# One triangle of X X^T and the zeros of unused rows, in a four-layer image kernel

## The reference, cut to what matters

```python
x = x + L0(_gn(x))   # 1x1 conv to 576, depthwise 3x3/5x5/7x7, 1x1 conv, channel attention with top-k, 1x1 conv
x = x + L1(_gn(x))   # below
x = x + L2(_gn(x))   # selective scan
x = x + L3(_gn(x))   # depthwise 7x7, mirrored borders

def L1(x, w_qkv):    # x: (2, 192, 64, 64), 8 heads of 24 channels
    qkv = jnp.einsum('bchw,oc->bohw', x, w_qkv)
    q, k, v = jnp.split(qkv, 3, axis=1)
    q = _l2norm(q); k = _l2norm(k)                    # over the pixels
    attn = softmax(jnp.einsum('bhcn,bhdn->bhcd', q, k) / sqrt(hw))
    return jnp.einsum('bhcd,bhdn->bhcn', attn, v)
```

## Time and profile before

| | us |
|---|---|
| median of 3 runs | 2481.89 (2481.35 to 2492.42) |
| profiled execution | 2484.08 |
| its span | 2482.2 |
| TensorE busy | 1941.6 (78%) |
| VectorE busy | 1276.3 (51%) |
| ScalarE busy | 804.2 (32%) |
| GpSimd busy | 856.1 (34%) |

### The profile page before, as it was taken

One profiled execution on the slowest core, in us unless ns is written; L12 is line 12 of the kernel. 1 busy time (PEld: TensorE's weight loads), 2 busy tenths in 40 slices (PEclk: granted clock), 3 DMA queues, 4 the chain that ended last, 5 costly groups with the idle time before them and its releaser, 6 DMA issues. The chain is left out here.

```text
span 2482.2 us, 36929 instructions
## 1 busy us (share of the span) xinstructions
PE 1941.6 (78%) x15660; PEld 1208.7 (49%) x15660; DVE 1276.3 (51%) x1317; ACT 804.2 (32%) x1269; POOL 856.1 (34%) x452
## 2 busy tenths in 40 slices
PE   3789899769999999999977867777677767775042
PEld 1477776667777777777734422222222222221032
DVE  5445454441111111111172055799999999998613
ACT  2345455440000000000042125733543444334610
POOL 3234333430000000000000040499899989994000
PEclk9889899889999999999988878899889988998565
DMA  8899999969242323221030031588778868873799
GB/s 292 264 347 318 345 326 345 357 214 242 63 117 62 105 75 93 87 82 39 1 102 11 0 116 44 133 204 213 183 198 221 214 163 220 210 187 108 206 293 309
DMA packets 205013, 441.32 MB, mean 178 GB/s; under 512 B 19728, under 2 KB 150800, under 8 KB 192432
## 3 DMA queue, kind: packets, MB, share of 16 engines
q1 hardware_dynamic: 180976, 426.47, 57.9%
q10 hardware_dynamic: 23872, 12.49, 1.8%
HBM read 309.65 MB, written 128.45 MB: 176 GB/s over the span
## 5 line engine op out<-in xcount | busy, mean ns | idle before, releaser
L755 PE MATMUL ps<-mem 128*128 128x288 f16 x5376 | 654.8, 287 | 9.6 <-DMA mem<-depthwise_out 9.6
L755 PEld LDWEIGHTS ps<-mem 128*128 128x128 f16 x5376 | 502.1, 98 | 148.2 <-issue 15.4
L1729 POOL TENSOR_TENSOR mem<-mem 128x1024 f32<-128x1024 f32 x192 | 465.5, 2441 | 45.3 <-ACT mem L1663 42.7
L1638 PE MATMUL ps<-mem 128*128 128x512 f32 x768 | 416.6, 675 | 39.4 <-POOL mem L1729 35.6
L540 PE MATMUL ps<-mem 56*96 56x240 f16 (+1 forms) x5184 | 314.8, 284 | 74.3 <-POOL mem L630 41.1
L1124 POOL TENSOR_TENSOR mem<-mem 128x1536 f16<-128x1536 f32 x16 | 50.8, 3179 | 928.7 <-ACT mem L1102 928.7
L540 PEld LDWEIGHTS ps<-mem 56*96 56x96 f16 x5184 | 305.4, 131 | 98.8 <-issue 56.6
L798 DVE TENSOR_TENSOR mem<-ps,mem 128x128 f16<-128x128 f32 x64 | 18.7, 292 | 586.9 <-ACT mem L819 586.9
L1758 DVE TENSOR_TENSOR_SCAN mem<-mem,ps 128x1024 f32<-128x1024 f32 x132 | 307.8, 2332 | 18.2 <-issue 10.3
L654 DVE TENSOR_TENSOR mem<-ps,mem 96x1024 f16<-96x1024 f32 x144 | 175.5, 1221 | 212.4 <-ACT mem L585 212.3
L1638 PEld LDWEIGHTS ps<-mem 128*128 128x128 f32 x768 | 153.5, 213 | 242.7 <-issue 133.7
(11 more groups left out here) (201 smaller groups left out, 1883.9 us busy)
## 6 DMA issues: line engine op xcount, KB each, us to landing
mem<-l_bc SPq DMA_DIRECT2D x504, 256.0 KB, 4.5
depthwise_out<-mem SPq DMA_DIRECT2D x35, 1536.0 KB, 10.8
mem<-depthwise_out SPq DMA_DIRECT2D x95, 512.0 KB, 6.2
mem<-base_phases SPq DMA_DIRECT2D x36, 1024.0 KB, 12.8
base_phases<-mem SPq DMA_DIRECT2D x112, 256.0 KB, 6.5
mem<-in_wd SPq DMA_DIRECT2D x36, 768.0 KB, 14.2
mem<-l_planes SPq DMA_DIRECT2D x12, 1152.0 KB, 8.4
mem<-depthwise_out SPq DMA_DIRECT2D x128, 64.0 KB, 6.0
```

The lines of the kernel that those rows point to most:

```text
L755: ins = nc.tensor.matmul(ps[:, 2 * (i % 2) + h, 0:HALF], d, pw[rows, wa, k, HALF * h:HALF * h + HALF], start=(k == 0 and n == 0), stop=(k ...
L1638: ins = nc.tensor.matmul(py[:, a, :], ident, hh[:, n % 4, 512 * a:512 * a + 512], start=(n % N == 0), stop=(n % N == N - 1))
L1729: nc.gpsimd.tensor_tensor(hh[:, n % 4, :], hh[:, n % 4, :], cs[:, n % 4, :], ALU.mult).then_inc(hc_pool, 1)
```

## The change

It has two parts that don't touch each other. The zeros are stored by one DMA for each t and tensor, as one contiguous stretch of DRAM cut into 128 equal pieces, one out of each partition of `ext`; the waits change from 96 to 32. In layer 1, the row block of 64 channels is multiplied with its own 64 columns alone, and the 64 x 128 block that is missing is made after the loop: two transposes of the upper right 128 x 64 block of each image into bank 0, and a copy each by ScalarE.

```diff
-    def store_unused(sp, t):
-        size = B * 2 * PLANE
-        src = ext[0:C // 2].rearrange("c s r n -> c (s r n)")[:, 0:(64 - TAPROWS) * size].rearrange("c (r n) -> c r n", n=size)
-        sp.dma_start(planes_d[t, TAPROWS:64].rearrange("r c b n -> c r (b n)"), src).then_inc(sem.unused_planes, 16)
+    def store_unused(sp, dst, done):
+        dst = dst.rearrange("(p n) -> p n", p=128)
+        sp.dma_start(dst, ext.rearrange("p s r n -> p (s r n)")[:, 0:dst.shape[1]]).then_inc(done, 16)
...
         for t in range(2):
-            for k in range(3):
-                sp.dma_start(base_d[t, TAPROWS:64, 96 * k:96 * k + 96].rearrange("r c n -> c r n"),
-                             ext[0:96, 0:2].rearrange("c a r n -> c (a r) n")).then_inc(rest_stored, 16)
-            store_unused(sp, t)
+            store_unused(sp, base_d[t, TAPROWS:64].rearrange("r c n -> (r c n)"), rest_stored)
+            store_unused(sp, planes_d[t, TAPROWS:64].rearrange("r c b n -> (r c b n)"), sem.unused_planes)
...
-            sp.wait_ge(rest_stored, 96)
+            sp.wait_ge(rest_stored, 32)
...
-            pool.wait_ge(rest_stored, 96)
+            pool.wait_ge(rest_stored, 32)
...
                         for rb, x0, _, n in parts(b):
-                            ins = nc.tensor.matmul(ps[0:n, 2 + rb, C * b:C * b + C], xt[:, j % 2, x0:x0 + n],
-                                                   xt[:, j % 2, C * b:C * b + C],
+                            c0, cn = (C * b, C) if rb == 0 else (x0, n)
+                            ins = nc.tensor.matmul(ps[0:n, 2 + rb, c0:c0 + cn], xt[:, j % 2, x0:x0 + n], xt[:, j % 2, c0:c0 + cn],
                                                    start=(j == 0 and b == 0), stop=(j == NB - 1), skip_group_check=True)
...
-            pe.wait_ge(xxout, 2)
+            pe.wait_ge(xxout, 1)
+            for b in range(B):
+                c0 = parts(b)[1][2]
+                ins = nc.tensor.transpose(ps[0:64, 0, 128 * b:128 * b + 128], xx[:, 2 * b, c0:c0 + 64], ident)
+            ins.then_inc(tsum, 1)
+            pe.wait_ge(xxout, 1 + 2 * B)
...
-            nc.scalar.copy(xx.rearrange("p (b r) c -> p b r c", b=B)[0:64, :, 1, :],
-                           ps[0:64, 3, 0:2 * C].rearrange("p (b c) -> p b c", b=B)).then_inc(xxout, 1)
+            for b in range(B):
+                _, x0, c0, n = parts(b)[1]
+                nc.scalar.copy(xx[0:64, 2 * b + 1, c0:c0 + n], ps[0:64, 3, x0:x0 + n]).then_inc(xxout, 1)
+            act.wait_ge(tsum, NB + 1)
+            for b in range(B):
+                c0 = parts(b)[0][2]
+                nc.scalar.copy(xx[0:64, 2 * b + 1, c0:c0 + 128], ps[0:64, 0, 128 * b:128 * b + 128]).then_inc(xxout, 1)
```

## The result

| | before | changed |
|---|---|---|
| median of 5 runs, us | 2487.0 (2481.35 to 2492.42) | 2509.36 (2507.63 to 2515.61) |
| profiled span, us | 2482.2 | 2505.7 |
| TensorE's mean granted clock | 0.891 | 0.868 |

The ratio is 1.010, 95% interval [1.008, 1.012]. (The median of before over five runs lies 5 us above that of the three runs shown earlier.) The forecast was 2458, range 2452 to 2469: wrong in its sign.

What follows compares the result with a forecast made beforehand. The prediction took SyncE's issuing of zeros to bound the start and TensorE to bound layer 1's loop; -11.0 - 13.4 + 0.7 = -23.7 us took the median from 2481.89 to 2458.2, range 2452 to 2469.

Steps and rivals of the forecast that it cites:

- Part 1: Start of layer 0: zeros stored in large pieces let the next block start earlier, -11.0 us, between -7 and -11.5.
- The tail's copies and transposes: Behind layer 1's loop: the added transposes and copies that make the missing block cost +0.7 us.
- rival 5: Layer 1's loop itself runs at the lower clock as its columns per us fall: +15, 2497 us; chance 2%.
- the sum's -13.4 us for the loop: Layer 1's loop: 32 turns x 4 records x 0.105 us saved by streaming 64 columns instead of 192.
- 0.82 ns a column, on a fixed part of 0.09: Layer 1's f32 matmuls: assumed time of a record at full clock, the fixed part in us; 128 columns fewer save 0.105.
- overlap rule: TensorE matmuls: weights of the next tile load while this tile's matmul runs; the prediction saw only partial agreement in the loop.
- 3.13 us for the eight records of the first turn: Layer 1's loop: first turn's L1208 records, taken as at clock 0.50, from which a half-clock turn of 2.86 us was worked out.
- Tail: Steps behind layer 1's loop: +7 us if the clock is low there, and +0.7 for the added copies and transposes.

Runs made afterwards that it cites:

- merged version: Changed kernel with one 128 x 128 matmul for the lower blocks of both images in place of two of 64 x 64; 2444.98 us, ratio 0.984.
- the one with wide tiles and all columns: Kernel before with the large stores of zeros and 128-wide weight tiles for the lower block, all streams of 192 columns; 2452.41 us, ratio 0.986.
- warm start: Changed kernel plus six needless f32 matmuls ahead of layer 1's loop; eight executions took 2500.0 to 2512.6 us, two 2462.7 and 2468.5.

## Why the prediction was wrong, step by step

**What held.** Part 1, in each of its steps: VectorE's chain ends the block (29.97 said, 30.00 seen), SyncE is done with the zeros long before 28, the rate is 422 GB/s (430 said), GpSimd's first shift waits for them (2.65 us, until 41.64; about 1 us, until 40.1, had been forecast), and the first depthwise matmul starts at 76.22 (near 77 said). Term: 11.0 said, 11.8 at that matmul, 12.6 in the medians of the run that has it alone (9.9 in its profiled span). The tail's copies and transposes: +0.7 said; in the merged version, at full clock, the first copy starts at 1353.85 and L1222's load at 1355.36, 1.51 us against 0.96, so +0.55.

**The step that failed** is rival 5, given 2%: "Against: TensorE never goes idle in the loop." It is what happened: the sum's -13.4 us for the loop, which took the clock of 1.00 as given, came out as +29.1. The sentence took the busy share of 15.00 in 15 us for proof that the array works all the time. It is not: in the same stretch the weight loads' own rows show an idle of 0.23 or 0.28 us at four places a turn, and with these pauses gone the same streams take 0.64 us less a turn, although TensorE counts as busy 100% in both. I used the starts of those loads and not what stood behind them in brackets. With the narrow tiles' streams cut to a third, what lay between those pauses got shorter, and the clock never rose. The Trainium skill (TensorE: Matmul & The Clock Gate, "Part 1: The HAM clock gate") says that activity sets the clock. No run here measures that activity; what the trace shows is that the profile's busy share doesn't stand for it, since the clock was 0.50 over 102 us that all count as busy.

**The term that was mis-sized**: "0.82 ns a column, on a fixed part of 0.09". The slope is right: 0.16 us for 192 columns in the merged version. The fixed part is not one of each record. It comes with the changes of the tile's width, and is 0 for 192 columns between tiles of one width. I had it from rows of 96-wide tiles, where the weight tiles change their rows from 128 to 64 partitions all the time (whether that is what costs there was not tested), and took the agreement with the 64-wide rows for a law of f32 matmuls. The overlap rule of the Trainium skill (TensorE: Matmul & The Clock Gate, "Step-by-step: what each phase is for") was then discounted as agreeing "only in part". In the merged version and the one with wide tiles and all columns the trace agrees with it, at 0.16 us a record, and the right question was why it did not in this loop.

**Rival 5's own price** was low: a turn of 2.86 us at half clock, 2497 in all; measured 3.23 and 2509. The step that failed in it is its starting point, 3.13 us for the eight records of the first turn "at 0.50". The clock rose within that turn; the last narrow loads already take 0.19 us, not 0.29. Two lines of before, the narrow loads of that turn:

```profile
1326.43 0.29 PEld L1208 LDWEIGHTS ps<-mem 128*64 128x64 f32 x2 [0.44 <-issue]
...
1328.17 0.19 PEld L1208 LDWEIGHTS ps<-mem 128*64 128x64 f32 x2 [0.40 <-issue]
```

From one to the other it is 1.74 us for a narrow and a wide pair, almost all of it at half clock; in the changed kernel 1315.74 - 1314.40 = 1.34. That is 0.20 saved by each short record, close to the 0.21 of the prediction. With 2 x 1.74 in place of 3.13 the same sum gives turns of 3.2 us. Tail: 7 and 0.7 said, +8.1 measured.

**Chances and range.** Nothing of the sum could catch an event whose size (some 45 us between turns of 1.84, an estimate, and of 3.23) was three times the gain at stake and whose chance rested on one misread number. The price had been worked out; its 2% had not.

**Open.** The runs do not show what exactly the clock looks at: four changes of width a turn with streams of 128 columns got 1.00, two with streams of 64 got 1.00, four with 64 got 0.50. Every edit that removed pauses also shortened the turn, so the pauses as such and the fewer columns per us stay two readings of the same runs. Nor do they show why two of ten executions with the warm start were some 40 us quicker than the others. Of the 3.5 us that part 1 gained between the first depthwise matmul and layer 1, and of what the run with the zeros alone lost again behind it, the cause was not looked for; later stages differ by a few us between all these runs.

## What to carry to other kernels

Read the weight loads' idle time, not the matmuls' busy share: when a row of loads shows idle "issue" in front of it at the changes of tile width, the loop may be losing time there, and the clock with it. The idle alone proves nothing: the needless matmuls of the warm start have 0.30 us of it in front of loads of one and the same tile, where each load (0.34 us) merely waits under a stream of 384 columns (one record every 0.64 us at half clock, and 384 columns at twice 0.82 ns are 0.63). Compare the time of a turn with its streams. Keep stationary tiles of one width next to each other, pad a narrow one to the full width when its surplus can be thrown away, or merge two; doing more arithmetic this way took 22 us off a 2474 us kernel. In these runs, putting the narrow tiles next to each other cost no arithmetic and saved the clock as well. Before cutting the columns of a stream, ask what clock the loop will have afterwards, and give that a chance of its own when the loop runs at the high level with pauses in it.

## What the runs showed of the hardware that I had not expected

- f32 matmuls with 128 x 128 weights and 192 columns follow each other at 0.16 us a record; with a 64-wide tile in between, the narrow load waits 0.23 us at full clock and 0.44 at half, and the wide load behind it 0.28 behind streams of 192 columns and 0.17 behind streams of 128 (at full clock).
- TensorE stayed at the lower of its two levels (1.2 of 2.4 GHz) for 102 us in which its matmul rows show no idle time.
- Four stores issued in 128 contiguous pieces each took SyncE 2.69, 2.10, 1.24 and 0.43 us, with 422 GB/s moved from 24 to 40 us; cut into pieces of about 1 KB, the same bytes held SyncE for 32 us, with 289 GB/s from 24 to 48.
